# Masked graph attention on one core: adjacency to 32-bit codes in one pass, scores in natural column order

## Chip, cores and metric

One Trainium2 chip; the kernel runs on one of its cores. The metric is the device time of one execution in microseconds (us). The kernel before was run three times: 925.25, 925.26 and 925.46 us.

## The reference, cut to what matters

```python
# x: 6144 x 128, adj: 6144 x 6144 int32 (zeros and ones), input: 6144 x 128, weight: 128 x 128
h = jnp.maximum(_layernorm(x, axis=-1), 0.0)
anchor_adj = jnp.einsum('md,de,ne->mn', h, weight, input)
scores = jnp.where(adj > 0, anchor_adj, -2 ** 32 + 1)
atten = jax.nn.softmax(scores / 0.07, axis=1)
out = x + atten @ input
```

## The kernel before

The 6144 rows of x are 48 tiles of 128 rows. A node is a row of `input`; there are 6144 of them, in 12 turns of 512. Four engines work on a tile, each from its own program; the tiles overlap, and semaphores tie the programs together.

**Head.** SyncE (SP) loads the nodes. They come in runs of four neighbouring nodes per partition (`nodes_v`), 2 KB each, so within a turn of 512 nodes partition p holds nodes 4p to 4p+3, and block b of the turn holds the nodes 4p+b. TensorE (PE) turns the blocks (L977) and multiplies them by the weight in fp32 (`make_y`, L961 to L968): y, 128 x 6144. ScalarE (ACT) and VectorE (DVE) split y into two fp16 halves (L592, L754). The columns of y are in block order, not in node order. The nodes also become the fp16 pair `v`: the high part on ACT (L574), the low part on GpSimd (POOL, L473 and L476) for parts 0, 2 and 3 and on DVE (`v_lo`, L758 to L765) for part 1, which turns 3, 4 and 5 use. The first tile's scores are interleaved with `make_y`.

**A step** of the main sequence works on tile t and on the tiles after it. `steps` (L304) runs steps 0 to 2 and the last five written out and the others in a loop. A step has three cycles; `P_AT`, `D_AT` and `S_AT` say by hand what stands where. In a cycle PE does, in this order: a transpose group of four blocks for turn k (`turn`, L910 to L925), a score chunk of 1024 columns for a later tile (`scores`, six matmuls at L900), the product of turn k (`product`, L927 to L952, eight matmuls at L948 and L950), a second group of transposes, its neighbour's product, a second score chunk, and two more products. DVE masks each score chunk (`mask`, L684 to L699): it takes the score from PSUM, subtracts `absent` (0 or 2 to the 64th), writes `probs` in SBUF and keeps the maximum. ACT takes the exponentials. Six of a tile's twelve turns (P halves) are transposed by PE: weights from `probs`, result in PSUM bank `ps_t`, high part by ACT (`hi_p`, L587), low part by DVE (`lo_p`, L718). The other six (D halves) get their exponentials into `ps_t` (L557), are split there by ACT (`hi_d`, L567) and DVE (`lo_d`, L724) into `split`, and are transposed by a DMA that SP issues (`turn_d`, L341 to L354). For the last tile POOL makes three of these splits out of SBUF (`split_d`, L479 to L491).

**The mask.** SP loads adj as three chunks of 2048 columns per tile, each once the chunk before in the same buffer has been read (`early_adj`, `next_adj`: waits on `present_done`). POOL makes two passes over each chunk: `find_present` (L441 to L452) writes bf16 flags in the order of adj, and `make_absent` (L454 to L461) reads them with a step of four elements, so that `absent` stands in block order, as the scores do. The second pass waits until DVE has masked the tile before (`masked`). Three of these second passes, chunk 1 of tile 1 and chunks 0 and 1 of tile 2, are made by ACT (`early_absent`, L595 to L600); the last two stand in step 0. In step 0 DVE's program also has the three `v_lo` instructions.

Of the kernel before, what the change touches and what calls it, by code (L numbers as in the profile page):

```python
# [5 lines left out]
def gnn_masked_attention_kernel(  # L6
# [15 lines left out]
    bf16 = mybir.dt.bfloat16  # L22
    fp16 = mybir.dt.float16
    int32 = mybir.dt.int32
    ALU = mybir.AluOpType
# [29 lines left out]
    H_SCALE = 2.0 ** 12  # L55
    Y_TOP = 14
    LEAST_Y_FIELD = 101
    ABSENT = 2.0 ** 64
# [24 lines left out]
    V_POOL = (0, 2, 3)  # L83
    V_VECTOR = (1,)
    FIRST_V_VECTOR = V_VECTOR[0] * (TURNS // PARTS)
# [16 lines left out]
    with ctx:  # L102
# [15 lines left out]
        absent = sb("absent", [P, CONVS, CONV], bf16)  # L118
        present = sb("present", [P, 2, CONV], bf16)
# [13 lines left out]
        w = sb("w", [P, D], fp32)  # L133
        wT = sb("wT", [P, D], fp32)
        minus_half = sb("minus_half", [P, 1], fp32)
        absent_top = sb("absent_top", [P, 1], fp32)
# [30 lines left out]
        spread_w = sb("spread_w", [P, P], fp32)  # L167
        spread_nodes = sb("spread_nodes", [P, P], fp32)
# [20 lines left out]
        top_set = sem("top_set")  # L189
        present_done = sem("present_done")  # L190
        absent_done = sem("absent_done")
        absent_early_done = sem("absent_early_done")
# [34 lines left out]
        v_lo_done = sem("v_lo_done")  # L227
# [64 lines left out]

        def by_block(part):

            return part.rearrange("q (g b p) -> q g b p", b=PER_TURN, p=P)

        def by_row(part):

            return part.rearrange("q (g p b) -> q g b p", b=PER_TURN, p=P)
# [17 lines left out]
        def _(sp):  # L317
# [79 lines left out]
        def _(pool):  # L397
            nc.gpsimd.memset(ident[:, :], 0.0).then_inc(ident_zero, 1)
            nc.gpsimd.memset(minus_half[:, :], -0.5).then_inc(half_done, 1)
            nc.gpsimd.memset(absent_top[:, :], ABSENT).then_inc(top_set, 1)  # L400
# [37 lines left out]
            def flags(s, c):  # L438
                return present[:, (s + c) % 2, :]

            def find_present(u, s, c):  # L441
                pool.wait_ge(adj_in[c], u * 16 + 16)

                if isinstance(u, int) and (u, c) in ((2, 0), (2, 2), (3, 0)):
                    pool.wait_ge(absent_early_done, {(2, 0): 1, (2, 2): 2, (3, 0): 3}[(u, c)])
                elif isinstance(u, int) and u == 2:
                    pool.wait_ge(absent_done, 2 * CONVS - 1)
                elif not (isinstance(u, int) and u < 2):
                    pool.wait_ge(absent_done, u * CONVS + (c - 4))
                pool.sem_inc(pool_waited, 1)  # L450
                nc.gpsimd.tensor_scalar(flags(s, c), adj_i[:, c, :], 1.0, 0.0, ALU.min, ALU.max)\  # L451
                    .then_inc(present_done, 1)  # L452

            def make_absent(u, s, c, free):  # L454
                pool.wait_ge(present_done, u * CONVS + c + 1)
                if free:
# [3 lines left out]
                nc.gpsimd.tensor_scalar(by_block(absent[:, c, :]), by_row(flags(s, c)), -ABSENT, ABSENT,  # L460
                                        ALU.mult, ALU.add).then_inc(absent_done, 1)  # L461

            def convert(u, s, c, free):
                find_present(u, s, c)
                make_absent(u, s, c, free)

            def v_lo_pool(n):

                i = V_POOL[n]
# [5 lines left out]
                pool.wait_ge(v_scaled, n + 1)  # L475
# [3 lines left out]
            def split_d(s, c):  # L479
# [7 lines left out]
                nc.gpsimd.tensor_scalar(split[:, d, 0, :], part, 1.0, 1.0, ALU.mult, ALU.mult)\  # L487
                    .then_inc(split_hi_done, 1)
                pool.wait_ge(split_hi_done, d // 2 + 1)
                nc.gpsimd.tensor_tensor(split[:, d, 1, :], part, split[:, d, 0, :],  # L490
# [4 lines left out]
            for c in range(CONVS):  # L495
                if c == 2:
                    pool.wait_ge(absent_done, 1)
                convert(0, 0, c, False)
            pool.wait_ge(absent_done, 2)
            find_present(1, 1, 0)  # L500
            pool.wait_ge(absent_done, 3)
            find_present(1, 1, 1)

            make_absent(1, 1, 0, True)
            v_lo_pool(0)
            pool.wait_ge(absent_done, 4)
            find_present(1, 1, 2)
            make_absent(1, 1, 2, True)
            make_h(2, 0)

            find_present(2, 0, 0)
            v_lo_pool(1)
            find_present(2, 0, 1)
            v_lo_pool(2)

            def step(t, par, at):
                if has(at, 2):
                    if at != 0:
                        convert(t + 2, par, 1, True)
# [3 lines left out]
                if has(at, 2):  # L523
                    convert(t + 2, par, 2, True)
                if has(at, 3):
                    convert(t + 3, 1 - par, 0, True)
# [9 lines left out]
        def _(act):  # L536
# [24 lines left out]
            def hi_d(u, c, g, n):  # L561
# [5 lines left out]
                nc.scalar.activation(split[:, d, 0, :], ps_t[n % BANKS][:, :], ACT.Copy)\  # L567
# [27 lines left out]
            def early_absent(u, c):  # L595

                act.wait_ge(present_done, u * CONVS + c + 1)
# [493 lines left out]
```

## Time and profile before

| | before |
|---|---|
| median of three runs | 925.26 us |
| span of the profiled execution, first to last instruction | 922.5 us |
| its own time by the runs shown (lowest to highest) | 925.25 to 925.46 us |
| PE busy | 906.1 us (98%) |
| DVE busy | 814.5 us (88%) |
| ACT busy | 744.0 us (81%) |
| POOL busy | 705.6 us (76%) |

The span is counted from the first instruction to the last; about 2.8 us of the measured time lie around it. The profiled execution has no separate time on its page, so the runs shown stand for it. Times in the rows below are counted from the start of the span. A matmul's record is longer than the distance to the next matmul, because matmuls are pipelined: PE's pace is read from the starts.

### The profile page before, as it was taken

Reading aid. Unit: us, or ns where it says so; the run is one execution under the profiler, and the core shown is the slowest. Engines: PE = TensorE matmul, PEld = TensorE weight load, DVE = VectorE, ACT = ScalarE, POOL = GpSimd, SP = SyncE. Lnnn points to the kernel's source line nnn. Section 1 sums busy time; section 2 is a strip of 40 time slices with the busy share of each in tenths; the row PEclk is TensorE's granted clock in tenths of the full one; section 3 lists DMA queues with packets and bytes.
Section 4 is the critical chain, followed back from the end, with each engine's and each line's share of the span. In section 5 each row is a group of like instructions: output and inputs, shape, how many; then the busy total and the mean of one; then the engine's idle time right before and its main releaser. Section 6 shows DMA issues by size and latency. Waiting matters only on the chain.

```text
span 922.5 us, 26099 instructions
## 1 busy us (share of the span) xinstructions
PE 906.1 (98%) x7566; PEld 659.9 (72%) x7566; DVE 814.5 (88%) x1626; ACT 744.0 (81%) x1468; POOL 705.6 (76%) x587
## 2 busy tenths in 40 slices
PE   7989999999999999999999999999999999999997
PEld 4466777777777777777777777777777777777776
DVE  6998889988998899889988998898889888988985
ACT  5987888888888888888888888888888888888885
POOL 5999878787778877887788778877887788788712
PEclk9999999999999999999999999999999999999999
DMA  9789999999999999999999999999999999999965
GB/s 343 232 224 257 279 267 278 257 287 266 286 278 267 272 273 273 267 272 273 276 273 267 269 274 274 275 260 276 276 268 265 276 274 278 260 270 269 278 105 100
DMA packets 360361, 242.46 MB, mean 263 GB/s; under 512 B 321808, under 2 KB 340368, under 8 KB 341904
## 3 DMA queue, kind: packets, MB, share of 16 engines
q1 hardware_dynamic: 353136, 238.87, 100.9%
q10 hardware_dynamic: 7200, 3.28, 1.5%
q8 instruction: 13, 0.21, 0.1%
q14 instruction: 12, 0.10, 0.0%
HBM read 160.50 MB, written 3.15 MB: 177 GB/s over the span
## 4 chain that ended last, share of the span: by engine, by line
PE 93%; DVE 2%; DMA 2%; SPq 2%; issue 1%; ACT 0%; DVEq 0%; ACTq 0%
PE ps_s L900 38%; PE ps_o L948 26%; PE ps_o L950 13%; PE ps_t L923 13%; DMA pT_dma<-split 2%; SPq L353 1%; PE ps_t L967 1%; DVE probs L695 1%; PE ps_s L977 1%; DMA nodes_raw<-in_L_gnn_input_dram 0%; DVE v L763 0%; DVE pT_lo L718 0%; DVE split L724 0%; PE ps_o L967 0%; DVE pT_hi L714 0%
## 5 line engine op out<-in xcount | busy, mean ns | idle before, releaser
L695 DVE CUSTOM_DVE_ANT_0 probs<-ps_s,absent 128x1024 f32<-128x1024 f32 x288 | 351.4, 1220 | 49.6 <-PE ps_s L900 42.8
L900 PE MATMUL ps_s<-yT_hi,hT 128*128 128x512 f16 x1152 | 389.2, 379 | 1.0 <-DVE chunk_max L695 0.9
L460 POOL TENSOR_SCALAR absent<-present 128x2048 bf16<-128x2048 bf16 x141 | 294.3, 2087 | 34.9 <-POOL present L451 34.3
L587 ACT ACTIVATE pT_hi<-ps_t 128x512 f16<-128x512 f32 x281 | 167.7, 597 | 156.0 <-PE ps_t L923 155.9
L451 POOL TENSOR_SCALAR present<-adj_i 128x2048 bf16<-128x2048 int32 x144 | 273.6, 1900 | 13.3 <-DMA adj_i<-in_adj_dram 13.3
L948 PE MATMUL ps_o<-v,pT_dma 128*128 128x256 f16 x1152 | 222.1, 273 | 5.2 <-DMA pT_dma<-split 2.9
L557 ACT ACTIVATE ps_t<-probs,neg_max,exp_scale 128x512 f32<-128x512 f32 x285 | 220.3, 773 | 2.6 <-DVE neg_max L705 1.2
L900 PE MATMUL ps_s<-yT_lo,hT 128*128 128x512 f16 x576 | 218.3, 379 | 0.0
L718 DVE TENSOR_TENSOR pT_lo<-ps_t,pT_hi 128x512 f16<-128x512 f32 x284 | 194.3, 684 | 21.8 <-ACT pT_hi L587 20.4
L948 PE MATMUL ps_o<-v,pT_hi 128*128 128x256 f16 x1152 | 205.9, 273 | 0.9 <-DVE pT_lo L718 0.8
L950 PE MATMUL ps_o<-v,pT_dma 128*128 128x128 f16 x1152 | 206.5, 220 | 0.0
L950 PE MATMUL ps_o<-v,pT_lo 128*128 128x128 f16 x1152 | 198.0, 219 | 0.0
L900 PEld LDWEIGHTS ps_s<-yT_hi,hT 128*128 128x128 f16 x1152 | 112.9, 98 | 108.1 <-DVE chunk_max L695 2.8
L724 DVE TENSOR_TENSOR split<-ps_t,split 128x512 f16<-128x512 f32 x285 | 182.5, 681 | 1.6 <-ACT split L567 1.5
L546 ACT ACTIVATE probs<-probs,neg_max,exp_scale 128x1024 f32<-128x1024 f32 x144 | 177.7, 1234 | 0.0
L923 PE MATMUL ps_t<-ident,probs 128*128 128x128 f32 x1136 | 172.8, 275 | 1.2 <-DVE split L724 1.1
L567 ACT ACTIVATE split<-ps_t 128x512 f16<-128x512 f32 x285 | 151.3, 580 | 0.0
L948 PEld LDWEIGHTS ps_o<-v,pT_dma 128*128 128x128 f16 x1152 | 113.1, 98 | 33.8 <-DMA pT_dma<-split 3.3
L948 PEld LDWEIGHTS ps_o<-v,pT_hi 128*128 128x128 f16 x1152 | 112.8, 98 | 29.3 <-DVE pT_lo L718 1.2
L950 PEld LDWEIGHTS ps_o<-v,pT_dma 128*128 128x128 f16 x1152 | 113.1, 98 | 17.6
L950 PEld LDWEIGHTS ps_o<-v,pT_lo 128*128 128x128 f16 x1152 | 112.9, 98 | 16.3
L923 PEld LDWEIGHTS ps_t<-ident,probs 128*128 128x128 f32 x1136 | 119.7, 141 | 5.3 <-DVE split L724 1.6
(82 smaller groups left out, 508.8 us busy)
## 6 DMA issues: line engine op xcount, KB each, us to landing
adj_i<-in_adj_dram SPq DMA_DIRECT2D x144, 1024.0 KB, 5.3
pT_dma<-split SPq DMA_TRANSPOSE x288, 3.5
nodes_raw<-in_L_gnn_input_dram SPq DMA_DIRECT2D x6, 512.0 KB, 6.7
x_res<-in_x_dram SPq DMA_DIRECT2D x48, 64.0 KB, 3.9
out_dram<-fin ACTq DMA_DIRECT2D x48, 64.0 KB, 2.5
x_ln<-in_x_dram SPq DMA_DIRECT2D x46, 64.0 KB, 5.0
hT<-h_split SPq DMA_TRANSPOSE x45, 5.0
x_ln<-in_x_dram ACTq DMA_DIRECT2D x2, 64.0 KB, 3.0
```

Of the source, the lines that this page charges most:

```text
L451: nc.gpsimd.tensor_scalar(flags(s, c), adj_i[:, c, :], 1.0, 0.0, ALU.min, ALU.max)\
L460: nc.gpsimd.tensor_scalar(by_block(absent[:, c, :]), by_row(flags(s, c)), -ABSENT, ABSENT, ALU.mult, ALU.add).then_inc(absent_done, 1)
L546: nc.scalar.activation(part, part, ACT.Exp, bias=neg_max[:, s, :], scale=exp_scale[:, :], accum_out=chunk_sum[:, s, c // 2:c // 2 + 1]).th ...
L557: nc.scalar.activation(part if n is None else ps_t[n % BANKS][:, :], part, ACT.Exp, bias=neg_max[:, s, :], scale=exp_scale[:, :], accum_ou ...
L587: nc.scalar.activation(pT_hi[:, p % BANKS, :], turn_area(k, at), ACT.Copy).then_inc(hi_done, 1)
L695: nc.vector.tensor_tensor_reduce(out=probs[:, s, j * SCORE:(j + 1) * SCORE], in0=ps_s[j % 2][:, :], in1=absent[:, c, part * SCORE:(part + ...
L718: nc.vector.tensor_tensor(pT_lo[:, p % BANKS, :], area, pT_hi[:, p % BANKS, :], ALU.subtract)\
L724: nc.vector.tensor_tensor(split[:, d, 1, :], ps_t[n % BANKS][:, :], split[:, d, 0, :], ALU.subtract).then_inc(turn_freed, 1)
L900: made = nc.tensor.matmul(ps_s[j % 2][:, q * 512:(q + 1) * 512], hT[:, s, part, :], y[:, cols], start=(part == 0 and y is yT_hi), stop=(pa ...
L923: made = nc.tensor.transpose(area[:, b * P:(b + 1) * P], probs[:, par, col:col + P], ident[:, :])
L948: nc.tensor.matmul(area[:, 0:2 * D], hi[b], v[:, blk, :, :].rearrange("p s d -> p (s d)"), start=(blk == 0), stop=(k == final and b == PER ...
L950: made = nc.tensor.matmul(area[:, 0:D], lo[b], v[:, blk, 0, :], start=False, stop=(k == final and b == PER_TURN - 1), skip_group_check=True)
```

## The change

- POOL makes one pass per chunk: `codes` = adj x (-2 to the 40th) + 2 to the 39th, written as uint32, in the order of adj. The value is outside uint32's range on both sides, so a code is the smallest or the largest value of the type. The pass waits for adj's landing and for `masked`; SP's loads of adj wait on its end (`coded`).
- `make_y` writes its PSUM bank with a step of four fp32 elements, so y, the scores, `codes` and `probs` are in node order. The scales of h and y change (`H_SCALE`, `Y_TOP`).
- The transposes of P halves read their weights from `probs` with a step of four elements; `hi_d` and `lo_d` read `ps_t` with that step and write `split` in block order; so do the three `split_d`, reading SBUF.
- ACT's three `early_absent` and DVE's three `v_lo` go; POOL makes the low part of `v` for all four parts, between its conversions.
- Four small head tensors share the space of one `pT_dma` buffer.

```diff
-    H_SCALE = 2.0 ** 12
-    Y_TOP = 14
+    H_SCALE = 2.0 ** -3
+    Y_TOP = 3
-    ABSENT = 2.0 ** 64
+    PRESENT_STEP = -2.0 ** 40
+    ABSENT = 2.0 ** 39
...
-        absent = sb("absent", [P, CONVS, CONV], bf16)
-        present = sb("present", [P, 2, CONV], bf16)
+        codes = sb("codes", [P, CONVS, CONV], uint32)
...
+        def by_key(part):
+            return part.rearrange("q (p b) -> q b p", b=PER_TURN)
         def by_block(part):
-            return part.rearrange("q (g b p) -> q g b p", b=PER_TURN, p=P)
+            return part.rearrange("q (b p) -> q b p", b=PER_TURN)
...
             def early_adj(n):
-                sp.wait_ge(present_done, n + 1)
+                sp.wait_ge(coded, n + 1)
...
                     if has(at, 3):
-                        sp.wait_ge(present_done, t * CONVS + (2 * CONVS + c + 1))
+                        sp.wait_ge(coded, t * CONVS + (2 * CONVS + c + 1))
...
+            def convert(u, c):
                 pool.wait_ge(adj_in[c], u * 16 + 16)
+                if not (isinstance(u, int) and u == 0):
                     pool.wait_ge(masked, u * SCORES + (PER_CONV * (c + 1) - SCORES))
                 pool.sem_inc(pool_waited, 1)
+                nc.gpsimd.tensor_scalar(codes[:, c, :], adj_i[:, c, :], PRESENT_STEP, ABSENT, ALU.mult, ALU.add)\
+                    .then_inc(coded, 1)
...
             for c in range(CONVS):
+                convert(0, c)
             v_lo_pool(0)
+            convert(1, 0)
+            v_lo_pool(1)
+            convert(1, 1)
+            convert(1, 2)
             make_h(2, 0)
+            convert(2, 0)
             v_lo_pool(2)
+            convert(2, 1)
+            v_lo_pool(3)
...
-                nc.scalar.activation(split[:, d, 0, :], ps_t[n % BANKS][:, :], ACT.Copy)\
+                nc.scalar.activation(by_block(split[:, d, 0, :]), by_key(ps_t[n % BANKS][:, :]), ACT.Copy)\
...
-                nc.vector.tensor_tensor(split[:, d, 1, :], ps_t[n % BANKS][:, :], split[:, d, 0, :],
-                                        ALU.subtract).then_inc(turn_freed, 1)
+                nc.vector.tensor_tensor(by_block(split[:, d, 1, :]), by_key(ps_t[n % BANKS][:, :]),
+                                        by_block(split[:, d, 0, :]), ALU.subtract).then_inc(turn_freed, 1)
...
-                    in0=ps_s[j % 2][:, :], in1=absent[:, c, part * SCORE:(part + 1) * SCORE],
+                    in0=ps_s[j % 2][:, :], in1=codes[:, c, part * SCORE:(part + 1) * SCORE],
...
-                    col = (k + 2) * TURN + b * P
-                    made = nc.tensor.transpose(area[:, b * P:(b + 1) * P], probs[:, par, col:col + P],
-                                               ident[:, :])
+                    keys = by_key(probs[:, par, (k + 2) * TURN:(k + 3) * TURN])[:, b, :]
+                    made = nc.tensor.transpose(area[:, b * P:(b + 1) * P], keys, ident[:, :])
...
-                nc.tensor.matmul(y_bank[k % Y_BANKS][:, :], wT[:, :], nodesT[:, k * TURN:(k + 1) * TURN],
+                nc.tensor.matmul(by_key(y_bank[k % Y_BANKS][:, :]), wT[:, :],
+                                 by_block(nodesT[:, k * TURN:(k + 1) * TURN]),
                                  start=True, stop=True).then_inc(y_made, 1)
```

## Rows read from the trace of the kernel before

**Rows 1.** The page: busy time by engine, us, share of the span, instructions.
```profile
PE 906.1 (98%) x7566; PEld 659.9 (72%) x7566; DVE 814.5 (88%) x1626; ACT 744.0 (81%) x1468; POOL 705.6 (76%) x587
```

**Rows 2.** Stretches: busy us of PE, PEld, DVE, ACT, POOL; granted clock, DMA share, GB/s.
```profile
52.20:55.60 3.40, 3.38 (x19) 2.58 (x20) 3.40 (x5) 1.03 (x2) 3.40 (x2) 0.51 1.04 201
440.00:458.35 18.35, 18.35 (x158) 13.50 (x156) 16.41 (x34) 15.02 (x31) 14.36 (x13) 1.00 1.05 271
```

**Rows 3.** Timeline of PE, transposes that begin two cycles of the loop: start, length.
```profile
444.81 0.61 PE L923 MATMUL ps_t<-ident,probs 128*128 128x128 f32 x4
...
450.93 0.61 PE L923 MATMUL ps_t<-ident,probs 128*128 128x128 f32 x4
```

**Rows 4.** Timeline of PE in step 0: start, length, idle time before and its releaser.
```profile
47.73 0.61 PE L923 MATMUL ps_t<-ident,probs 128*128 128x128 f32 x4
48.50 0.38 PE L900 MATMUL ps_s<-yT_hi,hT 128*128 128x512 f16 x1 [0.16 <-DVE hT L681]
...
52.22 0.39 PE L948 MATMUL ps_o<-v,pT_dma 128*128 128x256 f16 x1 [2.26 <-DVE v L763]
...
58.28 0.61 PE L923 MATMUL ps_t<-ident,probs 128*128 128x128 f32 x4
```

**Rows 5.** Queue of SP in step 0: four transposes issued, and landing times from 36 to 60 us.
```profile
42.74 4.90 SPq L353 DMA_TRANSPOSE pT_dma<-split  x2
...
49.41 3.76 SPq L353 DMA_TRANSPOSE pT_dma<-split  x2
...
DMA to landing us min/median/max: 3.2/4.7/6.1
```

**Rows 6.** Timeline of POOL and ACT in the head: the first low and high part of v.
```profile
33.25 1.55 POOL L473 TENSOR_SCALAR nodes_raw<-nodes_raw,scale_bits 128x1536 f32<-128x1536 f32 x1
34.88 3.11 POOL L476 TENSOR_TENSOR v<-nodes_raw,v 128x1536 f16<-128x1536 f32 x1
...
21.36 1.57 ACT L574 ACTIVATE v<-nodes_raw,scale_bits 128x1536 f16<-128x1536 f32 x1
```

**Rows 7.** Groups by line, whole span: busy us, mean ns, idle before and releaser.
```profile
L695 DVE CUSTOM_DVE_ANT_0 probs<-ps_s,absent 128x1024 f32<-128x1024 f32 x288 | 351.4, 1220 | 49.6 <-PE ps_s L900 42.8 <-issue 1.6
...
L460 POOL TENSOR_SCALAR absent<-present 128x2048 bf16<-128x2048 bf16 x141 | 294.3, 2087 | 34.9 <-POOL present L451 34.3 <-DVE chunk_max L695 0.6
...
L451 POOL TENSOR_SCALAR present<-adj_i 128x2048 bf16<-128x2048 int32 x144 | 273.6, 1900 | 13.3 <-DMA adj_i<-in_adj_dram 13.3
...
L724 DVE TENSOR_TENSOR split<-ps_t,split 128x512 f16<-128x512 f32 x285 | 182.5, 681 | 1.6 <-ACT split L567 1.5
...
L741 DVE SCALAR_TENSOR_TENSOR fin_a<-ps_o,inv_sum,x_res 128x128 f32<-128x128 f32 x48 | 16.8, 350 | 3.1 <-PE ps_o L950 2.5
...
L599 ACT ACTIVATE absent<-present,absent_top 128x2048 bf16<-128x2048 bf16 x3 | 6.6, 2208 | 0.6 <-DVE chunk_max L695 0.6
```

**Rows 8.** Timelines in the loop: POOL's pass over a chunk 2, and SP's next load there.
```profile
441.32 1.89 POOL L451 TENSOR_SCALAR present<-adj_i 128x2048 bf16<-128x2048 int32 x1
...
449.00 0.36 SPq L322 DMA_DIRECT2D adj_i<-in_adj_dram  x1
```

**Rows 9.** Timelines of PE's loads and matmuls, one transpose group in the loop: start, length.
```profile
441.04 0.42 PEld L923 LDWEIGHTS ps_t<-ident,probs 128*128 128x128 f32 x4
...
441.09 0.60 PE L923 MATMUL ps_t<-ident,probs 128*128 128x128 f32 x4
441.54 0.27 PE L948 MATMUL ps_o<-v,pT_dma 128*128 128x256 f16 x1
```

**Rows 10.** Timeline of PE in the head: two of the twelve make_y, two matmuls each.
```profile
21.80 1.02 PE L967 MATMUL ps_t<-probs,wT 128*128 128x512 f32 x2
22.66 1.02 PE L967 MATMUL ps_o<-probs,wT 128*128 128x512 f32 x2
```

**Rows 11.** Timelines of the last tile: POOL's last split, and PE's last product.
```profile
910.88 1.16 POOL L490 TENSOR_TENSOR split<-probs,split 128x512 f16<-128x512 f32 x1
...
918.74 0.27 PE L948 MATMUL ps_o<-v,pT_dma 128*128 128x256 f16 x1
```

More of the change, by code:

```diff
@@ L21, in gnn_masked_attention_kernel @@
     fp32 = mybir.dt.float32
[L22 removed]
     fp16 = mybir.dt.float16
     int32 = mybir.dt.int32
+    uint32 = mybir.dt.uint32
     ALU = mybir.AluOpType
@@ L166, in gnn_masked_attention_kernel @@
         exp_scale = sb("exp_scale", [P, 1], fp32)
-        spread_w = sb("spread_w", [P, P], fp32)
-        spread_nodes = sb("spread_nodes", [P, P], fp32)
+        head_only = pT_dma[:, D_HALVES - 1, :, :].rearrange("p b n -> p (b n)").bitcast(fp32)
+        w, wT, spread_w, spread_nodes = [head_only[:, i * P:(i + 1) * P] for i in range(4)]
         nodesT = probs[:, 1, :]
@@ L188, in gnn_masked_attention_kernel @@
         half_done = sem("half_done")
[L189 to L192, printed above, removed]
+        coded = sem("coded")
         stats_done = sem("stats_done")
@@ L436, in split_h, with v_lo_pool @@
                     .then_inc(h_split_done, 1)
-            def flags(s, c):
-                return present[:, (s + c) % 2, :]
-            def find_present(u, s, c):
+            def convert(u, c):
                 pool.wait_ge(adj_in[c], u * 16 + 16)
[L444 to L456, printed above, removed]
+                if not (isinstance(u, int) and u == 0):
                     pool.wait_ge(masked, u * SCORES + (PER_CONV * (c + 1) - SCORES))
                 pool.sem_inc(pool_waited, 1)
[L460 to L469, printed above, removed]
+                nc.gpsimd.tensor_scalar(codes[:, c, :], adj_i[:, c, :], PRESENT_STEP, ABSENT, ALU.mult, ALU.add)\
+                    .then_inc(coded, 1)
+            def v_lo_pool(i):
                 blocks = slice(i * PART, (i + 1) * PART)
@@ L518, in step @@
                     if at != 0:
-                        convert(t + 2, par, 1, True)
+                        convert(t + 2, 1)
                 if has(at, 3):
@@ L523, in step @@
                 if has(at, 2):
-                    convert(t + 2, par, 2, True)
+                    convert(t + 2, 2)
                 if has(at, 3):
-                    convert(t + 3, 1 - par, 0, True)
+                    convert(t + 3, 0)
                 if at == LAST - 1:
@@ L593, in y_hi @@
                                      scale=y_scale).then_inc(y_hi_done, 1)
-            def early_absent(u, c):
-                act.wait_ge(present_done, u * CONVS + c + 1)
-                act.wait_ge(masked, u * SCORES + (PER_CONV * (c + 1) - SCORES))
-                nc.scalar.activation(by_block(absent[:, c, :]), by_row(present[:, (u + c) % 2, :]), ACT.Identity,
-                                     bias=absent_top[:, :], scale=-ABSENT).then_inc(absent_early_done, 1)
             for u in range(2):
@@ L617, in _ @@
                     v_hi((k - 5) // 2)
-            act.wait_ge(top_set, 1)
-            early_absent(1, 1)
             for g in range(2):
@@ L633, in step @@
                 for z in range(CYCLES):
-                    if at == 0 and z > 0:
-                        early_absent(2, z - 1)
                     hi_p(t, CYCLE * z, at)
@@ L685, in mask @@
                 c = j // PER_CONV
-                if isinstance(u, int) and (u, c) in ((1, 1), (2, 0), (2, 1)):
-                    dve.wait_ge(absent_early_done, u + (1 if (u, c) == (2, 1) else 0))
-                elif isinstance(u, int) and u < 2:
-                    dve.wait_ge(absent_done, u * CONVS + c + (0 if (u, c) == (1, 2) else 1))
-                else:
-                    dve.wait_ge(absent_done, u * CONVS + (c - 2))
+                dve.wait_ge(coded, u * CONVS + (c + 1))
                 dve.wait_ge(scores_made, u * SCORES + (j + 1))
@@ L862, in step @@
                         invert_sum(t, par)
-                    if at == 0 and z == 1:
-                        v_lo(FIRST_V_VECTOR + 1)
                     lo_p(t, CYCLE * z, at)
-                    if at == 0 and z == 1:
-                        v_lo(FIRST_V_VECTOR + 2)
                     for q in range(2):
@@ L882, in step @@
                                 invert_sum(t, par)
-                            if at == 0 and z == 0:
-                                v_lo(FIRST_V_VECTOR)
             steps(dve, step)
@@ L928, in product @@
                 if at == 0:
[L929 to L933 removed]
+                    pe.wait_ge(v_lo_pool_done, k // PART_TURNS + 1)
                 if k in MULTIPLIED:
```

42 lines of the change are left out of this document (3 added, 39 removed).

## Prediction

> **What bounds the kernel now.** I read the page first, then the stretches, then PE's timeline where a stretch is not full. The page shows PE busy for 98% of the span, with DVE next at 88% and POOL at 76% [rows 1]. The stretch of one step of the loop says it plainly: of 18.35 us PE is busy for 18.35 at full clock, DVE for 16.41, ACT for 15.02, POOL for 14.36 [rows 2]. The timeline agrees: a cycle lasts 450.93 - 444.81 = 6.12 us, and three of them 18.35 [rows 3]. So in the loop POOL's time is worth nothing by itself. The change can only win where PE stands idle, and it loses wherever it slows PE, or another engine by more than its slack (1.94 us a step on DVE, 3.33 on ACT, 3.99 on POOL).
>
> PE's idle time is 922.5 - 906.1 = 16.4 us, most of it at the start, before data is there, and in the last tile. One piece is what the change touches: the second cycle of step 0 runs from 47.73 to 58.28, 10.55 us in place of 6.12 [rows 3, 4]. PE waits 2.26 us there for a low part of `v` that DVE makes [rows 4]. In the 3.4 us behind that wait the granted clock is 0.51, the lower of its two levels, 1.2 GHz [rows 2].
>
> **What the change does, part by part.**
>
> *The v_lo instructions leave DVE.* The excess of that cycle is 10.55 - 6.12 = 4.43 us. The 0.16 us before the scores, for hT, stay [rows 4]. The rest, 4.27 us, is the wait and the slow clock behind it: the product would be due at 48.50 + 1.29 (six score matmuls of 512 columns) = 49.8 and started at 52.22, 2.4 us later; 3.4 us at half clock lose 1.7 more. What is late next? This cycle's first two products need DMA transposes whose issue lies between 42.74 and 47.64; the second waits in the queue from about 44.2. At the slowest landing, 6.1 us, they are there at 48.8 and 50.3, and are due at 49.8 and 50.9 [rows 5]. The next two, issued from 49.41 and about 50.8 on, land by 56.9 at the slowest; product 9 would be due at 54.0 + 2.9 = 56.9. Covered, barely. Gain: 4.2 us.
>
> *POOL gets the whole of v's low part.* I rebuild its program. Before the first low part stand nine passes now and three afterwards; nine of 2 us end at 33.25, so they start near 15.2 and three are through at 21.5 [rows 6, 7]. v_lo_pool(0) then waits for ACT's high part, 21.36 + 1.57 = 22.93, and takes 1.55 + 3.11 plus gaps, 4.75 us: 27.7 [rows 6]. With 2.07 us for a pass (next paragraph): convert(1,0) to 29.8, v_lo(1) to 34.5, two passes to 38.7, make_h(2), some 2.5 us, to 41.2, convert(2,0) to 43.3, v_lo(2) to 48.1, convert(2,1) to 50.2, v_lo(3) to 55.0. PE wants part 1 at about 46.8, part 2 at 52.9, part 3 at 56.9. All in time, the last by 1.9 us. The codes come in time as well, a chunk some 3 us or more before DVE's mask.
>
> *One pass for two.* 1900 + 2087 ns a chunk become one pass [rows 7]. The trace has no pass of this size with a 32-bit result. Lower end: 1.9 us, the int32 read with a 16-bit result (L451). Upper end: 3.99 us, both passes together. The nearest row with a 32-bit result is L473, 1.55 us for 1536 elements [rows 6], by length 2.07 us for 2048; I take that. POOL is busy 3 x 1.9 us a step less, worth 0 in the loop, since PE is the cover; at the upper end POOL is no worse off than before. In step 0 there is no such cover: five passes stand between 22.93 and v_lo(3), so at the upper end it comes 5 x 1.92 = 9.6 us later, and PE waits.
>
> *Waits that move.* SP's loads of adj wait for `coded`, so for the only pass, and through it for `masked` of the tile before. Behind next_adj in SP's queue stand turn_d's transposes, for which PE waits. In the loop POOL comes to chunk 2 at 441.3 and SP asks for it at 449.0 [rows 8]; the mask it now waits for is a cycle old by then, so the code is there 5 us early; chunks 0 and 1 have more. In the head early_adj(4) asks for convert(1,1), ready at 36.6 by the list above, before the first split exists. Worth 0; if this cover were gone, each microsecond would delay transposes that have 0.6 us to spare in step 0.
>
> *ACT's three early_absent go*, 2208 ns each [rows 7]. Two stood in step 0, while PE waited for DVE or had work. Worth 0 beside the term above.
>
> *The mask reads 32-bit codes.* L695 takes 1220 ns, 1.05 ns an element and some 150 ns fixed; L741 reads PSUM and fp32, 350 ns for 128 elements, and shows no second slot per element [rows 7]. I take 0. Upper end: one more slot an element, 6 x 1.07 us a step, beyond DVE's slack; it would act like rival 3 and is counted there.
>
> *Steps of four elements.* Nothing in the trace moves with a step of 16 bytes. The nearest rows have 8 bytes: L460, 2087 ns against L451's 1900, and L599, 2208 ns for 2048 elements [rows 7]. A step costs 10% there at most. DVE and ACT read about one element a nanosecond; I take 0 for all uses. A gain is excluded. Upper ends:
> (a) PSUM reads of hi_d and lo_d: one more slot an element, 512 x 1.05 = 0.54 us on each of DVE's 681 ns [rows 7], and at most as much on ACT.
> (b) Weight loads, 24 a step: four loads lie within 0.42 us, four matmuls within 441.54 - 441.09 = 0.45 [rows 9]. Up to double, +0.10 us a load.
> (c) make_y's PSUM writes: a pair takes 22.66 - 21.80 = 0.86 us [rows 10]. Double is +0.86 on each of the last ten pairs, where PE's queue is full: +8.6 us.
> The last tile's three splits on POOL could double too: the last would end at 912.04 + 1.8 = 913.8, its transpose land at 918.5 by the median of 4.7, and PE's last product begins at 918.74 [rows 5, 11]. 0.
>
> **Sum.** 922.5 + 2.8 around the span = 925.3 us, which is the median of the runs; minus 4.2: **921.1 us**.
>
> **A page that speaks against the change.** make_y's fp32 matmuls start 0.43 us apart for 512 columns, 0.84 ns a column, with contiguous writes [rows 10]; no row has strided ones. The Trainium skill, "Advanced Engine Details and Errata", section Memory Cachelines, says that PSUM has 8-byte cachelines and that any non-contiguous pattern significantly slows matmuls. No run here shows it. By that rule the head would lose up to the 8.6 us of (c); without it, nothing.
>
> **Rivals.**
> 1. *make_y's writes slow down*, as in (c). PE's queue in the head has no idle time to hide it. 921.1 + 8.6 = 929.7 us; the gain is gone at 0.42 us a pair. Against: fp32 spends 0.84 ns on a column where the scores' fp16 spends 0.42, so the bank has twice the time for each write. Chance 0.12.
> 2. *Weight loads slow down*, the largest price on the other side. Place: the 1152 transposes. The gain is gone at 4.2 us / 1152 = 3.6 ns each. If only the first of a group shows (0.05 us x 288): +15, 936 us; with 0.10 us on each: +115, 1036 us. For: 0.42 of 0.45 us look taken. Against: 128 elements in 0.1 us is 0.8 ns for each step. Chance 0.12.
> 3. *Strided PSUM reads slow DVE.* 6 x 0.54 = 3.2 us a step against a slack of 1.94: a step of 19.6 us, 1.3 x 46 = +59, 980 us. It decides from 0.32 us an instruction on; below that PE hides it. Chance 0.10.
> 4. *POOL becomes what PE waits for in step 0.* If a pass takes over 2.07 + 1.9 / 5 = 2.45 us, v_lo(3) is late; at 2.9 us PE waits 2.3 us and the slow clock comes back: 923.5 to 926 us, no change. DMA transposes that come late there end the same way. Chance 0.12.
> 5. *As computed*, 921.1: 0.54.
>
> **How the numbers follow.** A measurement of this kernel can tell about 0.2%, 1.85 us, from no change. Case 5 is faster, case 4 is no change, cases 1 to 3 are slower, 0.34 together. The low end, 919, is case 5 with the first cycle of step 0 shorter too. The high end, 931, takes in cases 4 and 1; cases 2 and 3, 0.22, are nearly all left out. The likeliest case's own range is 919.5 to 923.
>
> **What would show it.** Right: the second cycle of step 0 lasts 6.1 to 6.5 us at clock 1.00, a loop step 18.35 us, four transposes 0.45 us, lo_d 0.68 us, a pass 2.0 to 2.2 us, and POOL's busy time is about 430 us. Wrong: a loop step over 18.4 us (the loads' or lo_d's duration then says which), make_y pairs over 0.9 us apart, or PE idle in step 0 on a release by POOL or a DMA.

## The result and the profile after

The changed kernel takes 942.63 us (942.08 to 945.64), the kernel before 925.26. The ratio is 1.0193, 95% interval 1.0182 to 1.0204: slower by 17.4 us. The forecast was 921.1 us, faster, and the range, up to 931, does not hold the result.

| | before | after |
|---|---|---|
| median | 925.26 us | 942.63 us |
| span of the profiled execution | 922.5 us | 940.8 us |
| PE busy, and idle in the span | 906.1, 16.4 us | 929.1, 11.7 us |
| POOL busy | 705.6 us | 422.2 us |
| one step of the loop | 18.35 us | 18.90 us |

Where the time and the span of one execution are both known, as here, they lie about 1.8 us apart (942.55 and 940.8 us). The 2.8 us that were taken for before compare its median with the span of an execution that was probably some 1 us shorter; that would be why the spans differ by 18.3 us and the medians by 17.4.

The page of the changed kernel, busy time by engine:

```profile
PE 929.1 (99%) x7566; PEld 685.2 (73%) x7566; DVE 810.6 (86%) x1623; ACT 738.0 (78%) x1465; POOL 422.2 (45%) x447
```

Against [rows 1], POOL has lost 283 us of work, DVE and ACT about 4 and 6, and PE has gained 23 us although it has the same 7566 matmuls. So PE does not wait more, it works more slowly. Which matmuls? The groups by line say it:

```profile
L640 DVE CUSTOM_DVE_ANT_0 probs<-ps_s,codes 128x1024 f32<-128x1024 f32 x288 | 351.7, 1221 | 57.8 <-PE ps_s L830 46.6
L434 POOL TENSOR_SCALAR codes<-adj_i 128x2048 uint32<-128x2048 int32 x144 | 275.0, 1910 | 309.0 <-DVE chunk_max L640 301.6
L669 DVE TENSOR_TENSOR split<-ps_t,split 128x512 f16<-128x512 f32 x285 | 182.6, 682 | 1.7 <-ACT split L528 1.6
L528 ACT ACTIVATE split<-ps_t 128x512 f16<-128x512 f32 x285 | 151.3, 580 | 0.0
L853 PE MATMUL ps_t<-ident,probs 128*128 128x128 f32 x1136 | 198.5, 297 | 1.0 <-DVE split L669 1.0
L853 PEld LDWEIGHTS ps_t<-ident,probs 128*128 128x128 f32 x1136 | 159.1, 210 | 5.0 <-DVE split L669 1.4 <-ACT probs L507 0.4
```

The mask and lo_d last what they did (1221 and 682 ns) [rows 7], and so does hi_d (580 ns, as in the same view of before). The one conversion pass takes 1910 ns, about as long as the first of the two old ones. What moved is the transposes of the P halves: a load of weights has gone from 141 ns (its mean in the same view of before) to 210, and the matmuls' busy time from 172.8 to 198.5 us.

PE's timeline gives the pace, here two groups that begin two cycles of the loop, and what follows the first of them, with their starts and lengths:

```profile
444.32 0.70 PE L853 MATMUL ps_t<-ident,probs 128*128 128x128 f32 x4
444.86 0.38 PE L830 MATMUL ps_s<-yT_hi,hT 128*128 128x512 f16 x1
...
450.62 0.70 PE L853 MATMUL ps_t<-ident,probs 128*128 128x128 f32 x4
```

A group of four takes 444.86 - 444.32 = 0.54 us, where it took 0.45 [rows 9]; a cycle 6.30 us, where it took 6.12 [rows 3]; a step 18.90. The four loads of this group, its first transpose alone, its last three, and the last three of the group of rows 9 in the kernel before:

```profile
444.27 0.56 PEld L853 LDWEIGHTS ps_t<-ident,probs 128*128 128x128 f32 x4
```

```profile
444.32 0.33 PE L853 MATMUL ps_t<-ident,probs 128*128 128x128 f32 x1
```

```profile
444.50 0.53 PE L853 MATMUL ps_t<-ident,probs 128*128 128x128 f32 x3
```

```profile
441.21 0.49 PE L923 MATMUL ps_t<-ident,probs 128*128 128x128 f32 x3
```

The loads lie within 0.56 us in place of 0.42 [rows 9]. Their records overlap, so that the second to fourth, 0.21 us long, come only some 0.12 us apart. The loss is not spread evenly. From the first transpose to the second it is 444.50 - 444.32 = 0.18 us, where it was 441.21 - 441.09 = 0.12 [rows 9]; the other three take 0.36 us together, where they took 0.33. The median distances of some 280 groups in each trace are 171, 121, 121 and 122 ns, where they were 115, 109, 109 and 109. So about 56 ns of a group's 92 are lost behind its first load, which has only a product's matmul of 128 columns ahead of it, and some 12 ns behind each of the others.

Step 0 is as forecast. Stretches of its second cycle and of one cycle of the loop, with the length, the busy us (instructions) of PE, PEld, DVE, ACT and POOL, the granted clock, DMA share and GB/s:

```profile
47.10:53.40 6.30, 6.30 (x55) 4.69 (x53) 5.62 (x14) 5.03 (x11) 6.22 (x3) 1.00 1.08 273
444.32:450.62 6.30, 6.30 (x55) 4.67 (x53) 5.23 (x11) 5.13 (x11) 3.70 (x5) 1.00 0.99 252
```

The second cycle of step 0 lasts exactly as long as one of the loop, PE full and at clock 1.00, where before it took 10.55 us with a stretch at 0.51 [rows 2, 4]. Step 1 begins at 60.03 in place of 64.40 us. PE's rows in the head and POOL's in step 0:

```profile
21.50 1.02 PE L892 MATMUL ps_t<-probs,pT_dma 128*128 128x512 f32 x2
22.36 1.02 PE L892 MATMUL ps_o<-probs,pT_dma 128*128 128x512 f32 x2
```

```profile
48.72 1.54 POOL L442 TENSOR_SCALAR nodes_raw<-nodes_raw,scale_bits 128x1536 f32<-128x1536 f32 x1
50.34 3.11 POOL L445 TENSOR_TENSOR v<-nodes_raw,v 128x1536 f16<-128x1536 f32 x1
```

A pair of make_y takes 0.86 us with strided writes, as it did without [rows 10]. The last low part of `v` is ready at 53.45.

So the difference of the spans, 18.3 us, is 23.0 more of PE's work less 4.7 of idle time that has gone. My theory (A): the step of four elements in the weight loads is the whole loss, and the rest of the change is worth what was forecast. Its rival (B): the loss comes from the codes that come later, the `masked` wait and SP's waits behind it.

### The profile page after: what moved, and what is told of

It reads as the page before. It is cut to its first block, busy times and chain, and to the rows that moved or that the text cites. A ratio compares the mean times of both kernels' runs of the same rounds, so it can differ in the third digit from the quotient of the medians.

```text
span 940.8 us, 25567 instructions
## 1 busy us (share of the span) xinstructions
PE 929.1 (99%) x7566; PEld 685.2 (73%) x7566; DVE 810.6 (86%) x1623; ACT 738.0 (78%) x1465; POOL 422.2 (45%) x447
## 4 chain that ended last, share of the span: by engine, by line
PE 95%; DVE 2%; DMA 2%; issue 1%; ACT 0%; SPq 0%; DVEq 0%; ACTq 0%
PE ps_s L830 38%; PE ps_o L873 26%; PE ps_t L853 16%; PE ps_o L875 13%; DMA pT_dma<-split 1%; PE ps_t L892 1%; DVE probs L640 1%; PE ps_s L903 1%; DMA nodes_raw<-in_L_gnn_input_dram 0%; DVE pT_lo L663 0%; PE ps_o L892 0%; DVE split L669 0%; PE ps_s L853 0%; DVE pT_hi L659 0%; SPq L344 0%
## 5 line engine op out<-in xcount | busy, mean ns | idle before, releaser
L434 POOL TENSOR_SCALAR codes<-adj_i 128x2048 uint32<-128x2048 int32 x144 | 275.0, 1910 | 309.0 <-DVE chunk_max L640 301.6
L640 DVE CUSTOM_DVE_ANT_0 probs<-ps_s,codes 128x1024 f32<-128x1024 f32 x288 | 351.7, 1221 | 57.8 <-PE ps_s L830 46.6
L853 PE MATMUL ps_t<-ident,probs 128*128 128x128 f32 x1136 | 198.5, 297 | 1.0 <-DVE split L669 1.0
L853 PEld LDWEIGHTS ps_t<-ident,probs 128*128 128x128 f32 x1136 | 159.1, 210 | 5.0 <-DVE split L669 1.4
L830 PEld LDWEIGHTS ps_s<-yT_lo,hT 128*128 128x128 f16 x576 | 56.4, 98 | 37.0 <-issue 1.3
```

Source lines behind the costliest of these rows:

```text
L434: nc.gpsimd.tensor_scalar(codes[:, c, :], adj_i[:, c, :], PRESENT_STEP, ABSENT, ALU.mult, ALU.add)\
L640: nc.vector.tensor_tensor_reduce(out=probs[:, s, j * SCORE:(j + 1) * SCORE], in0=ps_s[j % 2][:, :], in1=codes[:, c, part * SCORE:(part + 1 ...
L830: made = nc.tensor.matmul(ps_s[j % 2][:, q * 512:(q + 1) * 512], hT[:, s, part, :], y[:, cols], start=(part == 0 and y is yT_hi), stop=(pa ...
L853: made = nc.tensor.transpose(area[:, b * P:(b + 1) * P], keys, ident[:, :])
```

## The experiments

**1. The changed kernel with plain weights.**

```diff
-                    keys = by_key(probs[:, par, (k + 2) * TURN:(k + 3) * TURN])[:, b, :]
+                    keys = probs[:, par, (k + 2) * TURN + b * P:(k + 2) * TURN + (b + 1) * P]
```

> The changed kernel, but the P halves' transposes read their weights in blocks of 128 neighbouring columns again; everything else as changed. This pairs some probabilities with the wrong nodes, so part of the output differs; the work is the same. Theory A (the step of four elements in the weight loads is the whole loss): a group of four transposes takes 0.45 us instead of 0.54, a loop step 18.35 us instead of 18.9, the time falls by 288 x 0.09 = 26 us less what the slower pace had hidden, to 917 to 922 us, below the kernel before. Theory B (the loss comes from the later codes, the masked wait or the longer SP waits): stays near 942 us.

Measured: 921.58 us, ratio to before 0.9957 (0.9941 to 0.9974). One line takes back 21 us. A holds and B falls: all of B's waits are still in this kernel. Its groups by line:

```profile
L853 PE MATMUL ps_t<-ident,probs 128*128 128x128 f32 x1136 | 172.4, 274 | 1.2 <-DVE split L669 1.1
L853 PEld LDWEIGHTS ps_t<-ident,probs 128*128 128x128 f32 x1136 | 119.4, 140 | 5.3 <-DVE split L669 1.6 <-ACT probs L507 0.4
```

PE's work falls from 929.1 to 904.6 us, 24.5 us or 0.085 a group. Only 21.0 of it comes out of the span (940.8 to 919.8), because PE's idle time rises from 11.7 to 15.2: with slower transposes PE had come later to places where it otherwise waits for a DMA transpose (such waits are 0.7 us in the changed kernel and 4.2 in this one).

**2. The kernel before with strided weights alone.**

```diff
-                    made = nc.tensor.transpose(area[:, b * P:(b + 1) * P], probs[:, par, col:col + P],
+                    keys = probs[:, par, (k + 2) * TURN:(k + 3) * TURN].rearrange("q (p b) -> q b p", b=PER_TURN)[:, b, :]
+                    made = nc.tensor.transpose(area[:, b * P:(b + 1) * P], keys,
```

> The kernel before with one part of the change: the P halves' weights are read with a step of four elements. The probabilities of each such turn come out in another order, so the output differs; the work is the same. Theory A: a load record of 210 ns instead of 141, a group of 0.54 us, a loop step of 18.9 us, and 925.3 + 26 = 951 us, less 0 to 3 us. Theory B: 925 us.

Measured: 947.43 us, ratio 1.0247 (1.0228 to 1.0265), so +22 us, just under the 948 to 951 of theory A, with a load of 210 ns again. The same price from the other side. PE's work grows by 24.9 us (906.1 to 931.0) and the span by 23.0.

**3. The kernel before with the step in PSUM alone.**

```diff
-                nc.scalar.activation(split[:, d, 0, :], ps_t[n % BANKS][:, :], ACT.Copy)
+                nc.scalar.activation(split[:, d, 0, :].rearrange("q (b p) -> q b p", b=PER_TURN),
+                                     ps_t[n % BANKS][:, :].rearrange("q (p b) -> q b p", b=PER_TURN), ACT.Copy)
```

and the same in `lo_d`, and in `make_y` for the bank that is written and for `nodesT`.

> The kernel before with the other two uses of the step: ScalarE and VectorE read PSUM with a step of four fp32 for the D halves and the twelve y matmuls write PSUM with it. The order of nodes comes out wrong, the work is the same. From the changed kernel's trace (lo_d 682 ns, hi_d 580 ns, a y pair 0.86 us) both theories expect no change: 925.3 within 1 us, these three durations as before. The rule that a non-contiguous PSUM pattern slows matmuls would give up to +8.6 us.

Measured: 925.65 us, ratio 1.0003 (0.9993 to 1.0013). Its DVE and ACT rows:

```profile
L724 DVE TENSOR_TENSOR split<-ps_t,split 128x512 f16<-128x512 f32 x285 | 182.6, 682 | 1.6 <-ACT split L567 1.5
L567 ACT ACTIVATE split<-ps_t 128x512 f16<-128x512 f32 x285 | 151.6, 582 | 0.0
```

```profile
21.52 1.02 PE L967 MATMUL ps_t<-probs,wT 128*128 128x512 f32 x2
22.38 1.02 PE L967 MATMUL ps_o<-probs,wT 128*128 128x512 f32 x2
```

Here, reading PSUM with a step of 16 bytes costs DVE and ACT nothing, and writing it so costs an fp32 matmul of 512 columns nothing: a pair of make_y stays at 0.86 us.

**4. The changed kernel with v_lo back on DVE.** POOL's `v_lo_pool(1)` goes, and DVE has its three instructions again:

```diff
+                    if at == 0 and z == 1:
+                        v_lo(4)
                     lo_p(t, CYCLE * z, at)
+                    if at == 0 and z == 1:
+                        v_lo(5)
...
+                            if at == 0 and z == 0:
+                                v_lo(3)
```

> The changed kernel with the low part of v for turns 3 to 5 back on VectorE, in its three instructions at their old places; GpSimd makes the other three parts. If the gain of the change in step 0 was this move: the second cycle of step 0 gets its PE wait of about 2 us and the slow clock back, and the time rises by about 4.3 us, to 947. Rival: with GpSimd's second pass gone, VectorE's three instructions no longer meet GpSimd and take about 0.75 us each instead of 1.6 to 2.4, PE waits under 0.5 us, and the time stays within 1 us of 942.6.

Measured: 948.12 us, ratio to before 1.0245 (1.0228 to 1.0262), 5.5 us above the changed kernel, a little more than the 4.3 expected. The rival falls. The second cycle of step 0 and one of PE's waits in it, then DVE's and POOL's timelines there:

```profile
47.71:59.31 11.60, 8.47 (x54) 5.28 (x53) 10.26 (x18) 4.97 (x10) 7.82 (x7) 0.85 1.00 262
```

```profile
54.36 0.28 PE L891 MATMUL ps_o<-v,pT_dma 128*128 128x256 f16 x1 [2.14 <-DVE v L708]
```

```profile
49.75 1.04 DVE L708 SCALAR_TENSOR_TENSOR v<-nodes_raw,scale_bits,v 128x512 f16<-128x512 f32 x1
51.32 2.98 DVE L708 SCALAR_TENSOR_TENSOR v<-nodes_raw,scale_bits,v 128x512 f16<-128x512 f32 x1
```

```profile
50.34 3.41 POOL L446 TENSOR_TENSOR v<-nodes_raw,v 128x1536 f16<-128x1536 f32 x1
```

The cycle takes 11.60 us in place of 6.30, with a mean granted clock of 0.85. DVE's instruction that runs beside POOL's for 2.4 us takes 2.98 us; the one ahead of it, which meets it for 0.45 us, takes 1.04, and POOL's takes 3.41 in place of 3.11. So the two still meet, because POOL works on its own parts of `v` just then. The Trainium skill, "SBUF — State Buffer", section Who interferes with whom, says that DVE and GpSimd share one pair of SBUF ports under an exclusive lock. The trace agrees as far as it goes: both instructions read two operands from SBUF, and both are longer when they overlap.

**5 to 8. How the cost depends on the step.** The same line of `turn`, with other steps; a step of three only in three of a group's four loads.

```diff
+ step_two:   probs[turn].rearrange("q (h p c) -> q h c p", h=2, c=2)[:, b // 2, b % 2, :]
+ step_three: probs[:, par, base:base + 3 * P].rearrange("q (p c) -> q c p", c=3)[:, b, :]   # b < 3
+ step_six:   probs[:, par, base:base + 6 * P].rearrange("q (p c) -> q c p", c=6)[:, k % 2 * 2 + b, :]
+ step_eight: probs[two turns].rearrange("q (p c) -> q c p", c=8)[:, k % 2 * 4 + b, :]
```

> The changed kernel with the weights of the P halves' transposes read with a step of two elements, 8 bytes, in place of four; part of the output differs, the work is the same. If what costs is that each read takes a new 16-byte stretch of SBUF, two reads share one here, the load record stays near 141 ns, and the time is 921.6 as with plain weights. If any step costs the same, 210 ns and 942.6. If the cost grows with the step, about 163 to 175 ns and 928 to 932.

> The changed kernel with a step of eight elements, 32 bytes, over pairs of turns; part of the output differs, the work is the same. If the cost is one per read outside the last 16 bytes, it is the same as with four: a load of 210 ns, a group of 0.54 us, 942.6. If it grows with the step: 280 to 350 ns a load, and 965 or more.

> The changed kernel with three of the four weight loads of a group at a step of three elements, 12 bytes, and the fourth plain; part of the output differs. With loads of 208, 210 and 195 ns at steps of 2, 4 and 8, I have two theories. Any step but one costs the same because neighbouring pairs are read together only when plain: 208 to 210 ns. Or even steps meet on part of the memory and an odd step does not: 141 to 195 ns. For the time: 936 to 938 by the first, 922 to 933 by the second.

> The changed kernel at a step of six elements, 24 bytes; part of the output differs. By the first theory (any step the same, eight being the odd one out) 210 ns and 942; if the cost falls with the step beyond 16 bytes, between 210 and 195 ns and 936 to 942.

| step, elements (bytes) | load: min, median, max, ns | time, us | ratio to before |
|---|---|---|---|
| 1 (4) | 138, 140, 143 | 921.58 | 0.9957 (0.9941 to 0.9974) |
| 2 (8) | 194, 209, 219 | 941.55 | 1.0178 (1.0139 to 1.0216) |
| 3 (12), three of four | 144, 194, 214 | 936.37 | 1.0111 (1.0085 to 1.0138) |
| 4 (16) | 195, 212, 220 | 942.63 | 1.0193 (1.0182 to 1.0204) |
| 6 (24) | 209, 236, 242 | 957.52 | 1.0343 (1.032 to 1.0366) |
| 8 (32) | 185, 194, 209 | 934.51 | 1.0101 (1.0068 to 1.0135) |

```profile
L853 PEld LDWEIGHTS ps_t<-ident,probs x1136: 194/209/219, 39.3 to 926.9; 128*128 128x128 f32 x190
```

```profile
L854 PEld LDWEIGHTS ps_t<-ident,probs x1136: 209/236/242, 40.2 to 943.5; 128*128 128x128 f32 x190
```

```profile
L853 PEld LDWEIGHTS ps_t<-ident,probs x1136: 185/194/209, 39.4 to 918.8; 128*128 128x128 f32 x190
```

```profile
L853 PEld LDWEIGHTS ps_t<-ident,probs x3: 196/209/217, 440.4 to 440.6; 128*128 128x128 f32 x3
```

```profile
L855 PEld LDWEIGHTS ps_t<-ident,probs x3: 192/194/208, 442.0 to 442.2; 128*128 128x128 f32 x3
```

The rows are, in this order, all weight loads with a step of two, six and eight, and the first three loads of one group with a step of two and of three. A step of 8 bytes costs as much as one of 16, though two reads share a 16-byte stretch there.

My three forecasts for step two included this outcome; those for eight and for six did not include theirs (eight cheaper than four, six dearer than all).

The Trainium skill, "Advanced Engine Details and Errata", section Memory Cachelines, says that SBUF has 16-byte cachelines and that two hits in a line are needed for full rate. Step four, with one hit in a line, does cost what that rule warns of, and the prediction did not weigh it for the loads. But by it step two would have cost nothing, and its load takes 209 ns, so for weight loads the measurement decides against the rule as a whole.

On step three the first theory (any step the same) nearly holds. Its time is right, 936.37 us: 14.8 over the plain weights, three quarters of the 20.0 at step two. Its loads are a little shorter than the 208 to 210 ns it named. The table's 194 ns takes in the plain load of each group; by their place in the group the strided three have medians of 192, 212 and 198 ns, where step two has 196, 217 and 209. The second theory, 922 to 933 us, misses.

What the law is stays open. What is settled is that each step tried lengthens the record of a load by some 50 to 96 ns, and a step of one does not.

**9. One group woven.** Score matmuls stand between the transposes of each cycle's first group.

```diff
+                turn(t, par, k, at, (0,))
...
+                for i in range(6):
+                    score((par + ahead) % 2, j, i)
+                    if i < 3:
+                        turn(t, par, k, at, (i + 1,))
```

> The changed kernel, output unchanged: the four transposes of each cycle's first group stand one by one between the six score matmuls of 512 columns that followed them. If a strided load costs only what sticks out beside the matmul before it (0.11 us for a transpose, 0.215 for a score matmul), the woven group costs 0.45 us or less again: half of the 288 groups lose 0.09 us, 13 us together, 929 to 931. If a strided load holds up PE by itself, 942.6.

Measured: 939.1 us, ratio 1.0144 (1.0111 to 1.0176), 3.5 us less than the changed kernel and not 13. PE's weight loads, where such a group begins:

```profile
443.48 0.20 PEld L847 LDWEIGHTS ps_t<-ident,probs 128*128 128x128 f32 x1
443.54 0.16 PEld L830 LDWEIGHTS ps_s<-yT_hi,hT 128*128 128x128 f16 x1
443.71 0.20 PEld L847 LDWEIGHTS ps_t<-ident,probs 128*128 128x128 f32 x1
443.93 0.10 PEld L830 LDWEIGHTS ps_s<-yT_lo,hT 128*128 128x128 f16 x1
```

The first strided load has only a product of 128 columns to hide beside, and the score's load behind it is stretched from 0.10 to 0.16 us. The later ones are covered: PE starts the second, third and fourth transpose of this group at 443.92, 444.25 and 444.57, 0.32 to 0.33 us apart, as much as a score matmul and a transpose take together. The forecast had the loss spread evenly. But 56 of a group's 92 ns are lost behind its first load, and that one stays as it was; weaving takes back the 36 ns of the other three, 5 us over 144 groups. PE's work falls by 4.7 us (929.1 to 924.4), the time by 3.5.

**10. Both groups woven, a score matmul ahead of each transpose.**

```diff
                 for i in range(6):
                     score((par + ahead) % 2, j, i)
+                    if i < 4:
+                        turn(t, par, k, at, (i,))
...
-                    turn(t, par, k + 1, at)
                     product(t, par, k + 1, at)
-                    scores(t, par, k + 3, at)
+                    turn_and_scores(t, par, k + 1, k + 3, at)
```

> The changed kernel, output unchanged: both groups of each cycle are woven, and a score matmul of 512 columns (0.215 us) stands ahead of each transpose, so each strided load has one to hide beside; the second group's product goes ahead of the group. In the version with one group woven, the first transpose stood ahead of the first score matmul, and 0.05 us was lost there. If a strided load costs PE only what sticks out beside the matmul ahead of it: nothing sticks out, a cycle takes 6.12 us and the time is 920 to 924. If part of the load holds PE up whatever stands ahead: a cycle of 6.2 to 6.3 us, 930 to 942. A rival for a miss: the second group's high and low parts come too late for its product, and PE waits for VectorE.

Measured: 1005.49 us, ratio 1.0866 (1.0839 to 1.0893). Far slower, by the rival that was named. PE's timeline shows the loads hidden:

```profile
441.30 0.38 PE L830 MATMUL ps_s<-yT_hi,hT 128*128 128x512 f16 x1
441.52 0.27 PE L847 MATMUL ps_t<-ident,probs 128*128 128x128 f32 x1
441.63 0.38 PE L830 MATMUL ps_s<-yT_lo,hT 128*128 128x512 f16 x1
441.84 0.27 PE L847 MATMUL ps_t<-ident,probs 128*128 128x128 f32 x1
441.95 0.38 PE L830 MATMUL ps_s<-yT_hi,hT 128*128 128x512 f16 x1
```

A score and a transpose take 441.95 - 441.30 = 0.65 us for two pairs, 0.325 each, which is what they cost with plain weights. But PE's waits show the price of the new order:

```profile
PE ps_o L879 <- DVE pT_lo L663: 56.1, 142, 0.9
```

```profile
443.64 0.22 PE L881 MATMUL ps_o<-v,pT_lo 128*128 128x128 f16 x1
444.26 0.28 PE L879 MATMUL ps_o<-v,pT_hi 128*128 128x256 f16 x1 [0.40 <-DVE pT_lo L663]
```

In this place the next product starts 0.62 us behind the matmul before it, where 0.06 us is the pace: 0.56 us lost, of which the last record's own length hides 0.16 from the idle time. At 142 such places that is 80 of the 84 us that this kernel takes over plain weights. Once a cycle the product needs a low part that DVE has not finished, since the second group moved too close to its product. A transposed block is worth nothing before ACT and DVE have split it.

**11. A version that beats both: the P halves in natural order.** The turns that PE transposes (2, 3, 6, 7, 10, 11) are the odd parts of 1024 nodes. Their nodes are loaded in natural order, and their weights and y columns need no step.

```diff
+    nodes_n = nodes.rearrange("(j c p) d -> j p c d", c=1024 // P, p=P)
...
+                if i % 2 == 1:
+                    sp.dma_start(nodes_raw[:, blocks, :], nodes_n[i]).then_inc(nodes_in[i], 16)
...
-                    keys = by_key(probs[:, par, (k + 2) * TURN:(k + 3) * TURN])[:, b, :]
+                    keys = probs[:, par, (k + 2) * TURN + b * P:(k + 2) * TURN + (b + 1) * P]
...
+                place = by_block if k // 2 % 2 == 1 else by_key
```

> A version with the reference's output. The nodes of the P halves (every second part of 1024) are loaded in natural order, 512 bytes a run, and their y matmuls write without a step; so the P halves' weights are plain columns, and only the D halves keep the strided PSUM reads. If the weight loads are the whole loss: groups of 0.45 us and 921.6 plus what the shorter runs of half the node loads cost in the head, 0 to 3 us: 921 to 925. If the head's loads are much slower in 512-byte runs, as much as they doubled (6.8 us to landing), 925 to 930.

Measured: 920.89 us (919.57 to 922.25), ratio 0.9955 (0.9938 to 0.9973): 0.45% faster than before. The shorter runs cost nothing that can be told: its first group of step 0 starts at 40.20 us, that of plain weights at 40.02, and the time is not above that kernel's 921.58.

```profile
L857 PEld LDWEIGHTS ps_t<-ident,probs 128*128 128x128 f32 x1136 | 119.4, 140 | 5.2 <-DVE split L673 1.6 <-ACT probs L511 0.4
```

**12. The same with POOL's second pass put back.**

```diff
+                if not (isinstance(u, int) and u < 3):
+                    nc.gpsimd.tensor_scalar(adj_i[:, c, :], adj_i[:, c, :], 1.0, 0.0, ALU.min, ALU.max).then_inc(spare_done, 1)
+                    pool.wait_ge(spare_done, u * CONVS + (c + 1 - 3 * CONVS))
```

> The version with natural order for the P halves, and from tile 3 on a second GpSimd pass of the same size over each chunk ahead of the code pass (it clamps adj in place, values unchanged, output unchanged): GpSimd's time per step is what it was before the change. If GpSimd's saved pass is worth nothing in the loop: 920.9, within 1.5 us, with GpSimd near 75% busy. If it is worth something there: 925 or more.

Measured: 921.66 us, ratio to before 0.9962 (0.9948 to 0.9976), and POOL busy for 676.3 us, 74%. The interval overlaps that of experiment 11. The 255 us of POOL's work that are put back cost nothing that can be told.

## Why the prediction was wrong

*What bounds the kernel.* Right, and it decided the case: PE is full in the loop, so any slowing of PE counts 288 times over. POOL's saved pass is worth 0 (experiment 12).

*The step of four elements, (b), weight loads.* This is the step that failed. The text took "0 for all uses" from rows of POOL and ACT with 8 bytes, and put the weight loads aside as rival 2 at 0.12, with a price range that runs from 0.05 us on the first of a group only (+15 us) to 0.10 us on every transpose (+115 us). The load record grew by 70 ns, and on average 0.022 us of it stuck out on each of the 1152 transposes: 24.5 to 24.9 us of PE's work. About 0.056 us of a group's loss lies behind its first load, which is rival 2's lower case and some 16 us over 288 groups; the other three loads add 0.012 us each, some 10 us. The forecast gave the point at which the gain is gone as 3.6 ns a transpose, and said of the load that "0.42 of 0.45 us look taken". That row was the one to go by, for it left next to no cover. The argument set against it, 0.8 ns for each step, did not hold: strided loads come 0.12 us and more apart, not 0.11. The rows of POOL and ACT that spoke for 0 are of other engines, and they had shown 10% even at 8 bytes. 10% on a load is 14 ns; by the share that stuck out here, 22 of 70 ns, that alone would have been 4 ns a transpose and the whole gain.

*(a), PSUM reads, and (c), make_y's writes.* Taken at 0, and 0 measured (experiment 3). The rule of the Trainium skill, "Advanced Engine Details and Errata", section Memory Cachelines, that a non-contiguous pattern in PSUM slows matmuls, is not borne out here: experiment 3 has such writes and its time is that of before.

*The last tile's three splits on POOL.* Rightly put at 0 for the time, since PE waits no longer there, but the step itself is not free. POOL's high part, read from SBUF with a step of 16 bytes, takes 1126 ns where it took 618, and its low part 1414 where it took 1160. The rows of after and before:

```profile
L456 POOL TENSOR_SCALAR split<-probs 128x512 f16<-128x512 f32 x3 | 3.4, 1126 | 24.3 <-ACT probs L518 24.3
```

```profile
L487 POOL TENSOR_SCALAR split<-probs 128x512 f16<-128x512 f32 x3 | 1.9, 618 | 24.9 <-ACT probs L557 24.9
```

So the forecast's "A step costs 10% there at most", drawn from 8 bytes, does not hold for POOL at 16 bytes. The kernel of experiment 1 has these splits too, so nothing of the 21 us is theirs.

*The v_lo instructions leave DVE.* Right for the second cycle, which went from 10.55 us to the length of a loop cycle; experiment 4 gives 5.5 us for the move alone. But "covered, barely" was too bold for the DMA transposes behind it. With plain weights (experiment 1) a product of the third cycle waits for one:

```profile
53.76:60.84 7.08, 6.27 (x54) 4.42 (x53) 5.40 (x12) 4.96 (x11) 6.20 (x9) 1.00 1.23 252
```

```profile
56.47 0.27 PE L873 MATMUL ps_o<-v,pT_dma 128*128 128x256 f16 x1 [0.81 <-DMA pT_dma<-split]
```

The cycle takes 7.08 us in place of 6.12 (6.96 to 7.42 in the three kernels with plain weights and the rest of the change), so step 1 begins 3.56 us earlier than before, not 4.2. Against the before of the same runs, 925.14, the gain is 3.6 us.

*POOL's program in step 0.* Right, a little on the safe side: 1.91 us a pass for the 2.07 assumed, v_lo(3) ready at 53.45 for 55.0.

*Waits that move, the mask's 32-bit codes, early_absent.* Together 0 within a microsecond, as taken: experiment 1 holds all of them and takes 921.58 us against the sum's 921.1. They were not measured one by one.

*The sum.* All terms but one were right within a microsecond, taken together; the one at 0 was worth 21 us net. The range left out rival 2 altogether, although its smallest price, 936 us, lay 7 us below the result. With an unmeasured cost on the bounding engine the range should have reached those 936 us; even then it would have missed, because the lower case left out the three loads behind the first.

## What to carry to other kernels

When an engine is full, price a change first by what it does to that engine's own instructions, and read the slack between its paired streams: four loads in 0.42 us beside four matmuls in 0.45 warn that a longer load is a longer step. Look at each place in a group by itself, above all at the first, for the instruction ahead of it may cover less. A row from another engine is no evidence for this one; a cost that is unknown on the full engine belongs in the range, however small the chance. To reorder data for free, try the step in reads of PSUM, on an engine with time to spare, or in the load from memory (both cost nothing here, experiments 3 and 11), and choose the layout by which engine transposes which part.

## What the runs showed of the hardware

- An fp32 weight load of 128 columns from SBUF has a record of 140 ns with neighbouring elements in the groups of transposes, and 194 to 236 ns (medians) with a step of two to eight, not in order of the step: six is the longest, eight the shortest. Back to back, loads with a step of four come 0.12 to 0.13 us apart, and they are hidden whole beside a matmul of 512 columns (experiment 10). The record does not hang on the step alone: in the head of the kernel before, make_y's weights, neighbouring fp32 elements too, have means of 190 and 206 ns.
- Reading PSUM with a step of 16 bytes left 682 ns on DVE and 580 to 582 on ACT for 512 fp32 elements; writing it with that step left an fp32 matmul pair at 0.86 us.
- Reading SBUF fp32 with a step of 16 bytes took POOL from 618 to 1126 ns (tensor_scalar) and from 1160 to 1414 ns (tensor_tensor) for 512 elements.
- POOL's pass of 2048 int32 elements to uint32 takes 1910 ns, as much as to bf16 (1900).
- A slower stage on the bounding engine is partly paid by waits that vanish elsewhere: of 24.5 us of added work, 21.0 reached the span.
